# Softplus logs from PSUM, both C products on VectorE at each eighth step, x1 copied by ScalarE, and the norms' roots one plan step later

## The reference

```python
xz = einsum('bld,kd->blk', x, W_x)              # dt_raw (128), b_ssm (16), c_ssm (16)
dt = softplus(einsum('blr,dr->bld', dt_raw, W_dt) + b_dt)
d_a = exp(dt[..., None] * a)                    # a = -exp(A_log), 16 states
dbx = dt[..., None] * b_ssm[:, :, None, :] * x[..., None]
h = d_a_t * h + dbx_t                           # along 512 positions
y = einsum('bdn,bn->bd', h, c_t)
return y + x * D_param
```

## Time and profile before

| | us |
|---|---|
| three runs | 3006.03, 3007.59, 3013.62 |
| median | 3007.59 |
| profiled execution, its own time | 3010.63 |
| its span, first to last instruction | 3008.8 |
| scan stage, by GpSimd's C products | 41.8 to 1050.5 |
| busy of PE, DVE, ACT, POOL over the span | 2720.0, 1793.9, 1298.4, 1528.1 |

### The profile page before, as it was taken

How to read it: one execution, slowest core, us unless ns; L and a number is a source line. 1 busy time by engine, 2 the same in 40 slices (tenths; PEclk the granted TensorE clock), 3 DMA queues, 4 the chain that set the end, 5 groups by cost and what they waited for, 6 DMA issues and landing times.

```text
span 3008.8 us, 37440 instructions
## 1 busy us (share of the span) xinstructions
PE 2720.0 (90%) x13484; PEld 1436.8 (48%) x13484; DVE 1793.9 (60%) x3787; ACT 1298.4 (43%) x2689; POOL 1528.1 (51%) x944
## 2 busy tenths in 40 slices
PE   4668889988998879999969999999899999999998
PEld 2455555545555534443335555555544444444443
DVE  5899999999999952232246666665524444222222
ACT  4557586766757411111127767666712220111111
POOL 5999999989999902222135555554400001121211
PEclk7769999998999889999989999999999999999999
DMA  5443645546454479999930000001135324899997
GB/s 189 150 168 139 204 168 171 189 136 192 164 192 162 138 295 355 396 394 392 380 109 1 29 29 29 29 29 58 47 100 196 117 74 164 307 383 338 361 334 219
DMA packets 168234, 566.13 MB, mean 188 GB/s; under 512 B 22832, under 2 KB 24752, under 8 KB 167536
## 3 DMA queue, kind: packets, MB, share of 16 engines
q1 hardware_dynamic: 149904, 521.65, 46.7%
q0 software_dynamic: 17088, 40.90, 5.9%
q10 hardware_dynamic: 1056, 1.18, 0.1%
HBM read 487.89 MB, written 75.79 MB: 187 GB/s over the span
## 4 chain that ended last, share of the span: by engine, by line
PE 54%; ACT 2%; DVE 2%; POOL 2%; issue 1%; DMA 1%; POOLq 0%; SPq 0%; DVEq 0%; ACTq 0%
PE bank L1140 10%; PE bank L1166 5%; PE bank L1078 5%; PE bank L1043 5%; PE bank L1064 5%; PE bank L1191 5%; PE bank L1248 4%; PE bank L1225 3%; PE bank L1213 2%; PE bank L1237 2%; POOL arena L1947 2%; PE bank L1123 1%; PE bank L1179 1%; ACT arena L1770 1%; PE bank L1050 1%
## 5 line engine op out<-in xcount | busy, mean ns | idle before, releaser
L1851 POOL TENSOR_TENSOR arena<-arena 128x1024 f32<-128x1024 f32 x256 | 606.3, 2369 | 6.3 <-DMA arena<-scratch_bc 3.0
L1699 ACT ACTIVATE bank<-arena 128x512 f32<-128x512 f32 x512 | 346.6, 689 | 318.9 <-DVE arena L1337 200.5
L1947 POOL TENSOR_TENSOR arena<-arena 128x2048 f32<-128x2048 f32 (+3 forms) x128 | 297.1, 2324 | 275.9 <-DVE arena L1567 275.8
L993 PE MATMUL bank<-arena 128*128 128x128 f32 x2048 | 306.3, 303 | 141.7 <-POOL arena L1857 141.6
L993 PEld LDWEIGHTS bank<-arena 128*128 128x128 f32 x2048 | 260.4, 156 | 227.7 <-POOL arena L1857 181.8
L1770 ACT ACTIVATE arena<-arena 128x256 f32<-128x256 f32 (+3 forms) x512 | 287.2, 566 | 148.9 <-DVE arena L1558 125.2
L1857 POOL TENSOR_TENSOR arena<-arena 128x512 f32<-128x512 f32 x256 | 334.2, 1306 | 21.4 <-DVE arena L1337 21.3
L1337 DVE TENSOR_TENSOR_SCAN arena<-bank,arena 128x512 f32<-128x512 f32 x256 | 310.6, 1213 | 24.8 <-POOL arena L1851 18.6
L1140 PE MATMUL bank<-arena 128*64 128x352 f32 x2048 | 322.7, 468 | 0.0
L1337 DVE TENSOR_TENSOR_SCAN bank<-bank,arena 128x512 f32<-128x512 f32 x256 | 308.4, 1205 | 0.0
L1064 PE MATMUL bank<-arena 128*128 128x512 f32 x640 | 288.3, 593 | 9.1 <-ACT arena L1726 9.1
(11 more groups left out here) (145 smaller groups left out, 4161.3 us busy)
## 6 DMA issues: line engine op xcount, KB each, us to landing
arena<-scratch_bc SPq DMA_DIRECT2D x128, 1024.0 KB, 5.4
arena<-in_w_out SPq DMA_DIRECT2D x128, 768.0 KB, 15.3
arena<-in_w_gate SPq DMA_DIRECT2D x128, 704.0 KB
arena<-in_w_up SPq DMA_DIRECT2D x128, 704.0 KB
scratch_x<-arena SPq DMA_DIRECT2D x16, 1024.0 KB, 4.5
scratch_xn<-arena SPq DMA_DIRECT2D x15, 1024.0 KB, 4.1
arena<-scratch_x SPq DMA_DIRECT2D x44, 256.0 KB, 6.0
arena<-scratch_x SPq DMA_DIRECT2D x8, 1024.0 KB, 7.5
```

The costliest lines, as they stand in the source:

```text
L993: i = nc.tensor.matmul(y[:, t * P:(t + 1) * P], w[:, n, t * P:(t + 1) * P], p.ident, is_transpose=True, start=False, stop=g == GROUPS - 1 ...
L1699: nc.scalar.activation(bank[p.da_bank(k, n)][:, :], block_of(p.dt, b, c), ACT.Exp, scale=p.alog[:, c, state:state + 1]).then_inc(*p.decaye ...
L1851: nc.gpsimd.tensor_tensor(out=p.hb[k % HB], in0=over(block_of(p.dtx, b, c), 1, NG), in1=p.bc[k // 2 % NBC][:, 0], op=ALU.mult).then_inc(*p ...
L1947: nc.gpsimd.tensor_tensor(out=own, in0=own, in1=over(p.rden[:, k % 2, :], 2, width), op=ALU.mult).then_inc(*p.divided.up(k))
```

## The change

Softplus: `soft_ln` works by blocks of 512 columns and writes into a bank of the ring of three, which then has four more products per batch. `dt_sum` works by blocks too and adds SBUF and PSUM. Both products: at steps with k % 8 == 4, VectorE leaves both scans in PSUM and multiplies both with C, and GpSimd leaves out its product. x1: TensorE adds the raw x to the y bank through the identity, and ScalarE copies the bank out, three steps behind instead of two. Roots: in the tables `rstd` stands one step later. The dt projections move two or three steps up, and the softplus items of the second half one step; `dt_sum` joins `TAKERS`.

```diff
+BOTH_EVERY, BOTH_AT = 8, 4
-PREPARE = (("x_in", 4), ("stats_a", 7), ("stats", 8), ("rstd", 8), ("apply", 11))
-TURN_S, DTR, BC, DT = (13, 13, 14, 14), 16, 15, (21, 21, 22, 25)
-SOFT = (("soft_exp", (24, 28)), ("soft_ln", (26, 29)), ("dt_sum", (27, 30)), ("dtx", (28, 31)))
+PREPARE = (("x_in", 4), ("stats_a", 7), ("stats", 8), ("rstd", 9), ("apply", 11))
+TURN_S, DTR, BC, DT = (13, 13, 14, 14), 16, 15, (19, 19, 20, 22)
+SOFT = (("soft_exp", (24, 27)), ("soft_ln", (25, 28)), ("dt_sum", (26, 29)), ("dtx", (27, 30)))
...
-X1_BEHIND = 2
+X1_BEHIND = 3
...
+def dve_weighs_both(k):
+    return k % BOTH_EVERY == BOTH_AT
...
+            wait_x(b)
+            nc.tensor.matmul(y[:, :], p.ident, p.xin[s][:, :, c * P:(c + 1) * P], start=True, stop=False,
+                             skip_group_check=True)
...
-    def dt_sum(b, h):
-        V.wait_ge(p.soft_ln, b, h)
-        dt, soft = half_of(p.dt, b, h), half_of(p.dtx, b, h)
-        nc.vector.tensor_tensor(out=dt, in0=dt, in1=soft, op=ALU.add).then_inc(*p.dt_ready.up(b, h))
+    def dt_sum(b, c):
+        ring, dt = p.rings[0], block_of(p.dt, b, c)
+        V.wait_ge(p.soft_ln, b, c)
+        nc.vector.tensor_tensor(out=dt, in0=dt, in1=bank[ring.bank("soft", b, c)][:, :], op=ALU.add).then_inc(
+            *ring.taken_by["dve"].up("soft", b, c))
...
+        if both:
+            V.wait_ge(p.scanned, k, 0)
+            nc.vector.tensor_tensor(out=h[:, 0, :], in0=banks[0][:, :], in1=p.bc[k // 2 % NBC][:, 1, 0, :],
+                                    op=ALU.mult).then_inc(*p.weighted_first.up(k))
...
-    def soft_ln(b, h):
-        soft = half_of(p.dtx, b, h)
-        A.wait_ge(p.soft_exp, b, h)
-        nc.scalar.activation(soft, soft, ACT.Ln, bias=1.0).then_inc(*p.soft_ln.up(b, h))
+    def soft_ln(b, c):
+        ring = p.rings[0]
+        A.wait_ge(p.soft_exp, b, c // 2)
+        A.wait_bank(ring, "soft", b, c)
+        nc.scalar.activation(bank[ring.bank("soft", b, c)][:, :], block_of(p.dtx, b, c), ACT.Ln, bias=1.0).then_inc(
+            *p.soft_ln.up(b, c))
...
+            elif before >= 0 and dve_weighs_both(before):
+                A.wait_ge(p.weighted_first, before)
...
+    def x1(b, c):
+        A.wait_ge(p.y_summed, step_at(b, c, GROUPS - 1))
+        nc.scalar.copy(p.xin[b % 2][:, :, c * P:(c + 1) * P],
+                       bank[Y_BANKS[c % 2]][:, :].rearrange("p (t d) -> p t d", t=QT)).then_inc(*p.x1_added.up(b, c))
...
     def weigh_c(k):
+        if dve_weighs_both(k):
+            return
```

More of the change, by code:

```diff
@@ L123, in __init__ @@
         self.index = {k: i for i, k in enumerate(products)}
-        self.made = Signal(prog, name + "_made", products)
+        self.made = Signal(prog, name + "_made", [k for k in products if k[0] != "soft"])
         self.taker = {k: e for k, e in takes}
@@ L276, in prepare_track @@
         for name, at in SOFT:
-            yield at[h], (name, b, h)
+            for key in soft_keys(name, h):
+                yield at[h], (name, b, key)
 def first_track():
@@ L285, in first_track @@
     for name, at in FIRST_SOFT:
-        yield at, (name, 0, 1)
+        for key in soft_keys(name, 1):
+            yield at, (name, 0, key)
 def quad_track(q):
@@ L320, in first_steps @@
     plan += [("dt", 0, 0), ("dt", 0, 1), ("dt_out", 0, 0), ("dt_out", 0, 1)]
-    plan += [("soft_exp", 0, 0), ("soft_ln", 0, 0), ("dt_sum", 0, 0), ("dtx", 0, 0)]
+    plan += [(name, 0, key) for name, _ in FIRST_SOFT for key in soft_keys(name, 0)]
     plan += [("x_in", 1), ("ff_w", 0), ("pads", 0)] + [("feed", k) for k in range(AHEAD)]
     return plan
-TAKERS = ("turned", "dtr_out", "bc_out", "dt_out", "logit", "folded", "silu", "hid", "so")
+TAKERS = ("turned", "dtr_out", "bc_out", "dt_out", "dt_sum", "logit", "folded", "silu", "hid", "so")
 def scan_plan():
@@ L818, in semaphores @@
         self.fed = sig("fed", "feed")
-        self.weighted = {"pool": sig("weighted_pool", "weigh_c"), "dve": sig("weighted_dve", "scan")}
+        self.weighted = {"pool": sig("weighted_pool", "weigh_c", where=lambda k: not dve_weighs_both(k)),
+                         "dve": sig("weighted_dve", "scan")}
+        self.weighted_first = sig("weighted_first", "scan", where=dve_weighs_both)
         self.y_summed = sig("y_summed", "sum")
@@ L977, in dt, with wait_x @@
                          start=True, stop=True).then_inc(*ring.made.up("dt", b, c))
+    def wait_x(b):
+        if b > 0:
+            PE.wait_ge(p.x_in[b % 2], b)
+            return
+        for t in range(QT):
+            PE.wait_ge(p.x_first[t], 0)
     def y_sum(k):
@@ L1332, in scan @@
         h = p.hb[k % HB]
-        banks = [bank[p.da_bank(k, n)] for n in range(NG)]
+        banks, both = [bank[p.da_bank(k, n)] for n in range(NG)], dve_weighs_both(k)
         V.wait_ge(p.fed, k)
```

40 lines of the change are left out of this document (21 added, 19 removed).

## The result

The changed kernel takes 3014.6 us (median of 12 runs, 3011.0 to 3019.1), the kernel before, beside it, 3008.0: a ratio of 1.0027, 95% interval 1.0019 to 1.0035 (the quotient of the two medians is 1.0022). It is a little slower; the forecast was 2988. One of the twelve executions of the kernel before took 4628.9 us and stands alone. The two profiled executions hide even the small loss: 3011.0 us (span 3009.1) against 3010.6 (span 3008.8). So the traces can tell where the expected 20 us went, and not all of the last few.

A forecast was written before the change was run, and what follows sets the result against it. VectorE was taken to bound batches 2 to 7, GpSimd batches 0 and 1. 736 + 15 - 2 = 749 gains 5 us, plus 14 in batches 0 and 1: 2988 us, own range 2979 to 2997, chance 0.42.

The forecast's parts named there:

- dt_sum: Softplus sum on VectorE, batches 2 to 7: with one PSUM operand 13.6 us instead of 28.3, -14.7.
- x1 and both products on VectorE: VectorE's work in batches 2 to 7: -16.3 us for x1 leaving, +16.6 for GpSimd's product taken every eighth step.
- ScalarE's waits: New waits for ScalarE, batches 2 to 7: late roots, joined table switches and a small x1 allowance, 15 us together.
- Other holds: Other two-SBUF operations on VectorE, batches 2 to 7: shorter holds, between 0 and 9 us, taken as 2.
- Neither is on the path by its mean: x added on TensorE (16 us) and copied by ScalarE (32 x 0.6 us) fits into idle time and costs nothing.
- rival B: No change: ScalarE waits twice the 15 us, or TensorE's queue at step 20 delays GpSimd's feed; 3005 us, chance 0.20.
- The x product: TensorE's added 128x512 matmul of x for each of 32 blocks: some 0.5 us each, 16 us.
- Batches 0 and 1: GpSimd leads there and is relieved: a gain of 15 us, 1 given back, so 14.
- the scan's own norm: Step 9, with roots a step later: the sum leaves over 2 us to spare.
- VectorE leads alone: Batches 2 to 7 without waits: VectorE 736 us, GpSimd 694.5, so GpSimd's relief is worth nothing there.
- C: Slower, through late roots and joined table switches with GpSimd lagging: 7.5 us a batch, +17, 3024 us, chance 0.15.
- Rival A: ScalarE's waits don't appear because it runs further ahead: 2971 us, or 2958 with all 9 of shorter holds; chance 0.23.

The follow-up runs named there:

- E14: Kernel before with softplus as ln(1 + exp(v)) and no sum, x1 by ScalarE, both C products each eighth step, roots at old steps: 2978.0 us, ratio 0.9891.
- E15: E14 without VectorE taking both C products each eighth step: 2982.4 us, ratio 0.9900.
- E5: Changed kernel with the shared products from the third on issued later, in all quads but the last: 3025.7 us, ratio 1.0051.
- E11: E1 with the quad norm's statistics and roots at step 2 and its apply at 4: 3008.0 us, ratio 0.9997.
- E1: Changed kernel with the inverse roots back at their old steps: 3008.3 us, ratio 1.0003.
- E9: Kernel before with only x1 changed, x through TensorE and copied out by ScalarE: 3012.0 us, ratio 1.0013.

## Why the prediction was wrong

- **dt_sum, right.** -14.7 forecast, -15.6 measured, and no long one: 32 of 675 to 686 ns. The Trainium skill (SBUF — State Buffer, "Who interferes with whom") says that a VectorE instruction with at most one SBUF input, outside the 2-port perf modes, doesn't contend with GpSimd; these 32 agree.
- **x1 and both products on VectorE, right.** -15.6 and +16.1 for -16.3 and +16.6.
- **ScalarE's waits, right.** 15 forecast, 14.7 measured: 2.2 us in even batches (1.5 of it at step 4, through the late roots) and 3.9 in odd ones (2.0 at step 26, 1.3 at step 29).
- **Other holds, right in sign.** Taken as -2; the 128x256 group fell from 11.4 to 5.7, the 128x4 group L1424 rose from 2.4 to 5.0.
- **"Neither is on the path by its mean", the step that failed.** It priced x through TensorE and the copy on ScalarE by their busy time in idle thirds. But the copy is a link between the last sum of a batch and the statistics that VectorE reaches at step 1, and a link is priced by when its input comes. The forecast never asked what stands ahead of that sum on TensorE: five shared products and the other sums, 21 us of work in one piece, for which the held dt_sum had left time. Taking the holds away took that time away, and the softplus products in the three banks added waits of up to 2.7 us a batch. The last sum came 10.4 us after the next batch's first scan for 5.0, and VectorE waited 13.4 us at the statistics and 6.3 at the shared product: 19.7 us that no term held. E14 and E15, without softplus in the ring, keep 8.0 and 14.6 of it. 749 was forecast for batches 2 to 7, 761.2 came, since other items gave some back. That these 19.7 us are the price of the miss is not shown: where order alone took them away (all in E5, 13.4 of them in E11), other waits and longer instructions came in their place. TensorE's ring was in rival B, at step 20 and for GpSimd; it struck at step 29 and for VectorE.
- **The x product was mis-sized too.** 0.5 us a block forecast; each block is two passes, 0.86 us from the start of the first to TensorE's next product (294.60 to 295.46 at the start of batch 2):

```profile
L1010 PE MATMUL bank<-arena x64: 592/593/1222, 34.6 to 1007.4; 128*128 128x512 f32 x64
```

- **Batches 0 and 1, half right.** 14 forecast, 8.4 measured. GpSimd's relief is there; ScalarE's new waits were taken as 1 and are 8.8 us (10.7 for 1.9). The forecast gave the scan's own norm over 2 us to spare; batch 0 waits 3.78 us behind it. With the roots back (E1) the two batches gain the 14.
- **"VectorE leads alone", right but not enough.** Even a VectorE with less work gains nothing while it waits: E9 gave it 14.5 us and lost them.
- **The rivals.** By size the result is B's, no change within 0.3%; in time, 3014.6 lies midway between B (3005) and C (3024). C's late roots are real, 6 us by E1. Rival A's 2958 does not come out of its terms: 18, 15 and 9 us off 3007.6 are 2966; nothing else hangs on it.

## What to carry to other kernels

When work moves to an idle engine, follow the value, not the busy share: write down what stands ahead of its producer and which engine reaches its consumer first. An engine with idle time on average can have none in one stretch: add up its work there, and ask whether a wait elsewhere was what left it time. When a rotation of three banks gets new users, list for each user the step in which its bank is freed. If a wait moves on when its cause is hidden, stop reordering and take a link away: here a sum that the formula didn't need was worth 30 us, more than any order gave.
